# Attention 1 stores undivided columns and sums of exponentials; the division moves to the last stage, and the attention runs in turns of three half tiles

## The chip, the cores and the metric

The kernel runs on one core of a Trainium2 chip. The metric is the device time of one execution in microseconds (us). Three executions of the kernel before took 2754.67, 2756.57 and 2761.1 us; their median, 2756.57, is the time before.

Five engines work at once, each through its own queue in order: TensorE (PE in the profile; PEld are its weight loads), VectorE (DVE), ScalarE (ACT), GpSimd (POOL) and SyncE (SP), which issues all DMAs here. They wait for each other through semaphores only.

## The reference, cut to what matters

```
x = x + xattn_0(layernorm(x), ctx)                 # fake-quantised projections
x = x + ffn_0(layernorm(x))
x = x + xattn_1(layernorm(x), ctx, mask)
x = x + ffn_1(layernorm(x))

def xattn_1(hidden, audio, mask):                  # 16 heads of 32, 4 batches of 512 rows, 1601 context tokens
    q, k, v  = heads(hidden @ Wq.T + bq), heads(audio @ Wk.T + bk), heads(audio @ Wv.T + bv)
    scores   = clip(q k^T / sqrt(32), -50, 50);  -50 where masked
    probs    = softmax(scores);  probs = probs / (probs.sum(-1) + 1e-8)
    ctx      = probs v                              # (4, 512, 512)
    delta    = clip(residual_scale, 0, 0.3) * (ctx @ Wo.T + bo)
    return layernorm(delta) * gamma + beta

def ffn_1(x):   # 8 experts, top 2; every expert has the same weights
    return relu(x @ W_up.T) @ W_down.T + sum(softmax(top2(x @ W_gate.T))) * (x @ W_expert)
```

All is float32 outside and has to be accurate to nearly that; products of float32 are made of three products of high and low parts.

## The kernel before

The program has five stages with a barrier between them: (1) keys, values and queries, (2) attention 0, (3) `ffn_0_and_q_projection_1`, (4) `attention_1`, (5) `out_projection_and_ffn_1`. The change touches stages 3 to 5. The order on every engine is written out by hand; generators (`projected`, `queries`, `closing`) are stepped beside a main loop, one step a `next`, and each engine walks through the same steps.

**Stage 3** (L1366 on) works through 4 batches of 16 slices `f` of the hidden layer. In slice `f` each engine makes `first_half(f + 1)`, steps its side work once, makes `second_half(f)` and steps it once more, so there are 30 steps a batch and a rest after the last. The side work of batch `b` is `projected(b + 1)`, the output projection of attention 0 for the next batch, and `queries(b - 1)`: the norm of the finished rows on DVE into `xn` (in the profile `q_rows`), 16 transposes of `xn` on PE, the split of the transposed rows into parts on ACT and DVE, 12 empty steps, and the query projection of attention 1. On PE and ACT `queries` starts with 6 empty steps; the norm on DVE takes 5 steps and one empty one stands behind it. The PSUM banks of this work (four, `hidden`) are taken in turns, always the one taken longest ago.

**Stage 4**, `attention_1` (L1814), works through 16 units, one for 4 heads of one batch, each of 13 tiles of 128 context tokens (the last has 65). A tile is two halves of 2 heads. For each half PE makes two score products into one of three PSUM windows of two banks (L1905), DVE clips them from PSUM into `probs` (L2009), and ACT takes the exponential in place (L1964). Two tiles later PE multiplies the tile with the values (L1918, four column tiles of 32 into bank `acc`). The sum of exponentials has two ways: for the tiles in `POOLED` (0, 1, 3, 5, 7, 9, 11) POOL adds the whole tile to `pooled` (L2040, six additions a unit), and PE makes one product of `pooled` with ones (L1937); for the six other tiles PE multiplies each with ones (L1931). Six buffers hold `probs`: tile i is clipped only when tile i - 6 has been read by PE and, if it is pooled, by POOL. A unit is closed during the next one: ACT copies `acc` and the sums (L1970, L1971), PE turns the sums into columns (L1883), DVE inverts them with one Newton step (L1986 to L1991), PE spreads the inverses again (L1893), and DVE multiplies (L1998); SP stores the columns to `o_t_1`. SP loads the next unit's keys, queries and values, and in the last unit the weights, rows and columns (`o_first`) of the last stage (`ahead`).

**Stage 5**, `out_projection_and_ffn_1` (L2087), has 4 batches. `projected(b)` splits the attention columns into parts (ACT L2219, DVE L2268), multiplies them with `Wo` on PE (48 products), adds and scales (DVE L2280, L2283), norms, multiplies by gamma and adds the rows (to which POOL has added beta, L2374), and norms again. Each norm has four short DVE instructions on 128x4 elements behind a POOL instruction (`root_on_pool`, L215) and four on 128x512 (L204). `operand(b)` transposes and splits the normed rows; then come gate, up, expert and down products. `projected(0)` and `projected(1)` stand ahead of the loop on PE; on DVE `projected(b + 1)` is stepped beside batch b.

## Time and profile before

| | us |
|---|---|
| median of three executions | 2756.57 |
| the profiled execution, its own time | 2758.67 |
| its span, first to last instruction | 2756.8 |
| PE busy | 2583.9 |
| DVE busy | 1842.0 |
| ACT busy | 1248.4 |
| POOL busy | 1204.4 |

Times in the rows are from the start of the span. A row of the timeline gives start and duration of a run of equal instructions (x8 is eight of them); in brackets stands how long the engine had been idle and who released it. Stage 3 lies between about 1445 and 1934 us, stage 4 from 1934 to 2516 us, stage 5 from there to the end. An f32 product appears as two instructions in the trace. A line number can be that of a helper.

### The profile page before, as it was taken

Reading aid. Unit: us, or ns where it says so; the run is one execution under the profiler, and the core shown is the slowest. Engines: PE = TensorE matmul, PEld = TensorE weight load, DVE = VectorE, ACT = ScalarE, POOL = GpSimd, SP = SyncE. Lnnn points to the kernel's source line nnn. Section 1 sums busy time; section 2 is a strip of 40 time slices with the busy share of each in tenths; the row PEclk is TensorE's granted clock in tenths of the full one; section 3 lists DMA queues with packets and bytes.
Section 4 is the critical chain, followed back from the end, with each engine's and each line's share of the span. In section 5 each row is a group of like instructions: output and inputs, shape, how many; then the busy total and the mean of one; then the engine's idle time right before and its main releaser. Section 6 shows DMA issues by size and latency. Waiting matters only on the chain. (4 is left out here: it accounts for less than half of the span.)

```text
span 2756.8 us, 35478 instructions
## 1 busy us (share of the span) xinstructions
PE 2583.9 (94%) x14009; PEld 1671.8 (61%) x14024; DVE 1842.0 (67%) x2545; ACT 1248.4 (45%) x1869; POOL 1204.4 (44%) x298
## 2 busy tenths in 40 slices
PE   8999999998999999999978998997999999997898
PEld 8888888885444444544426777776333434334776
DVE  5554544456676766767764766553899999997664
ACT  3222312214656565665642222222778778883211
POOL 1000000005999999999940000000677777774110
PEclk9999999999999999999999999999999999998899
DMA  8677666564534435344107534436967777762100
GB/s 294 239 232 258 251 228 246 176 192 116 122 68 93 97 65 121 67 97 93 62 4 256 191 134 164 150 118 167 191 150 152 150 153 150 153 186 100 62 31 31
DMA packets 214855, 400.61 MB, mean 145 GB/s; under 512 B 16696, under 2 KB 92504, under 8 KB 214624
## 3 DMA queue, kind: packets, MB, share of 16 engines
q1 hardware_dynamic: 214688, 398.34, 51.9%
q8 instruction: 111, 1.82, 0.3%
q14 instruction: 56, 0.46, 0.1%
HBM read 256.31 MB, written 140.33 MB: 144 GB/s over the span
## 5 line engine op out<-in xcount | busy, mean ns | idle before, releaser
L1300 POOL TENSOR_TENSOR pooled<-pooled,probs 128x2048 f32<-128x2048 f32 x140 | 641.1, 4579 | 22.1 <-ACT probs L1174 2.5
L1174 ACT ACTIVATE probs<-psum 128x512 f32<-128x512 f32 (+1 forms) x832 | 459.3, 598 | 373.4 <-PE psum L1071 370.4
L1201 DVE TENSOR_REDUCE win_max<-psum 128x1 f32<-128x802 f32 x480 | 453.7, 987 | 169.8 <-PE psum L1036 169.6
L2009 DVE TENSOR_SCALAR probs<-psum,bound 128x1024 f32<-128x1024 f32 (+1 forms) x416 | 507.4, 1277 | 44.5 <-PE psum L1905 44.5
L1964 ACT ACTIVATE probs<-probs 128x1024 f32<-128x1024 f32 (+1 forms) x416 | 440.6, 1059 | 113.3 <-DVE probs L2009 75.4
L2040 POOL TENSOR_TENSOR pooled<-pooled,probs 128x2048 f32<-128x2048 f32 x80 | 368.3, 4604 | 80.5 <-ACT probs L1964 80.5
L1071 PE MATMUL psum<-q_st,k_st 128*128 128x512 f32 (+1 forms) x832 | 336.8, 439 | 36.1 <-ACT den_sb L1186 17.9
L1071 PEld LDWEIGHTS psum<-q_st,k_st 128*128 128x128 f32 (+1 forms) x832 | 149.4, 186 | 258.5 <-ACT probs L1174 175.7
L215 POOL TENSOR_TENSOR r_q<-ve_q,minus_half 128x4 f32<-128x4 f32 x8 | 8.7, 1086 | 669.8 <-DVE ve_q L191 669.8
L1036 PE MATMUL psum<-k_st,q_st 96*128 96x402 f32 x960 | 266.6, 359 | 6.4 <-DVE o_sb L1232 5.2
L1905 PE MATMUL psum<-q_st,k_st 128*128 128x512 f32 (+1 forms) x832 | 250.8, 423 | 11.0 <-PEq L156 10.5
L1905 PEld LDWEIGHTS psum<-q_st,k_st 128*128 128x128 f32 (+1 forms) x832 | 137.4, 185 | 184.3 <-issue 93.5
L1083 PE MATMUL psum<-probs,v_st 128*32 128x512 f32 (+1 forms) x1664 | 222.5, 607 | 0.0
L1036 PEld LDWEIGHTS psum<-k_st,q_st 96*128 96x128 f32 x960 | 174.3, 191 | 61.2 <-DVE win_max L1201 31.6
L168 PE MATMUL psum<-q_st,k_st 128*128 128x512 f32 x576 | 174.4, 397 | 1.5 <-DVE early_v L1631 1.5
L168 PE MATMUL psum<-w,f_g_hi 128*128 128x512 f32 x512 | 165.0, 404 | 10.3 <-DVE f_g_lo L1675 7.3
L1576 ACT ACTIVATE f_code<-f_code 128x512 f32<-128x512 f32 x64 | 40.5, 632 | 288.9 <-DVE f_code L1673 288.9
L1300 POOL TENSOR_TENSOR pooled<-probs 128x2048 f32<-128x2048 f32 x16 | 73.4, 4588 | 198.3 <-ACT probs L1174 198.3
L786 DVE TENSOR_TENSOR v_out<-psum,bv 128x512 f32<-128x512 f32 (+1 forms) x104 | 70.9, 688 | 127.4 <-PE psum L168 115.6
L215 POOL TENSOR_TENSOR r_f<-ve_f,minus_half 128x4 f32<-128x4 f32 x11 | 11.1, 1012 | 328.2 <-DVE ve_f L191 328.2
L168 PE MATMUL psum<-ctx_hi,k_st 128*128 128x400 f32 (+1 forms) x512 | 139.2, 351 | 13.4 <-DVE ctx_lo L758 13.3
L650 ACT ACTIVATE kt_hi<-psum,bk 128x400 fp32r<-128x400 f32 (+1 forms) x128 | 74.6, 595 | 164.2 <-PE psum L168 164.0
(252 smaller groups left out, 4373.6 us busy)
## 6 DMA issues: line engine op xcount, KB each, us to landing
k_st<-k_hi SPq DMA_DIRECT2D x64, 801.0 KB, 11.8
k_st<-k_lo SPq DMA_DIRECT2D x48, 801.0 KB, 11.4
k_hi<-kt_hi SPq DMA_DIRECT2D x32, 801.0 KB, 4.0
k_lo<-kt_lo SPq DMA_DIRECT2D x32, 801.0 KB, 5.8
v_rows<-v_out SPq DMA_DIRECT2D x96, 256.0 KB
v_st<-v_rows SPq DMA_DIRECT2D x24, 768.0 KB
q_st<-q_hi SPq DMA_DIRECT2D x64, 256.0 KB, 11.0
w<-w_hi_d SPq DMA_DIRECT2D x64, 256.0 KB, 3.1
```

Of the source, the lines that this page charges most:

```text
L168: m = M.matmul(dst, lhs, rhs, start=start and n == 0, stop=stop and n == len(terms) - 1)
L650: A.activation(kt_hi[s][:, c0:c0 + cw], bank(kv_banks.where[i])[:, 0:cw], ACT.Identity, bias=bk[n][:, g:g + 1]).then_inc(k_hi_done, 1)
L1036: m = M.matmul(window(slot)[:, w, 0:MW], q_st[s][0:96, j, r * P:(r + 1) * P], k_st[s][0:96, j, start:start + MW], start=True, stop=True)
L1071: M.matmul(bank(slot)[0:rows, :], k_st[s][:, j, t * P:t * P + rows], q_st[s][:, j, :], start=True, stop=True).then_inc(scored, 1)
L1083: m = M.matmul(acc[j * DH:(j + 1) * DH, :], v_st[u % 2][0:rows, t, j * DH:(j + 1) * DH], pr[0:rows, j, :], start=(t == 0), stop=(t == TT - 1))
L1174: A.activation(probs[i % NPROBS][0:rows, j, :], bank(score_banks.where["score", u, t, j])[0:rows, :], ACT.Exp, scale=1.0 / ROOT).then_inc( ...
L1201: V.tensor_reduce(win_max[:, r, j, c:c + 1], window(windows.where["max", u, i])[:, :, 0:MV], AX.XY, ALU.max).then_inc(max_done, 1)
L1300: G.tensor_tensor(pooled[u % 2][:], before[:], probs[tile(u, k) % NPROBS][:], ALU.add).then_inc(pool_added, 1)
L1905: m = M.matmul(ps[0:rows, w, :], k_st[s][:, j + w, t * P:t * P + rows], q_st[s][:, j + w, :], start=True, stop=True)
L1964: A.activation(dst, dst, ACT.Exp, scale=1.0 / ROOT).then_inc(exp_done, 1)
L2009: V.tensor_scalar(probs[i % NPROBS][0:rows, half * W:half * W + W, :], window(("score", u, t, half))[0:rows], bound[0:rows, u // NG, t:t + 1],
L2040: G.tensor_tensor(pooled[:], before[:], this[:], ALU.add).then_inc(pool_added, 1)
```

## The change

It has five parts.

1. **Attention 1 no longer divides.** `closing` is gone on PE and DVE, with `rec`, `unity` and `o_sb`. ACT copies `acc` as soon as the last values product is made (`accumulated`) and the sums after the pooled product, in two places (`ACC_COPY`, `DEN_COPY`) instead of one. SP stores both: the undivided columns to `o_t_1`, the sums (4 rows of 512) to `den_d`. `pooled` has two buffers.
2. **Inverses by batch.** When a batch's four units are stored, SP loads its 8192 sums as 128x64, DVE takes the reciprocal, POOL makes the Newton step (`invert_on_pool`, three instructions), and SP stores them to `rec_d`. This is done for three batches in units 5, 9 and 13 and for the last in stage 5.
3. **Turns of three half tiles.** PE makes the scores of three halves in a row, then one or two value products with their sums (`VALUES`), nine turns a unit instead of 13 tiles of one step each.
4. **Seven pooled additions.** `POOLED` has eight tiles, so POOL makes seven additions a unit and PE five sums and the pooled one. The last unit has five additions and then, on POOL, the multiplication of `o_first` with the loaded inverses.
5. **Last stage and stage 3.** In stage 5 POOL multiplies the columns of batches 1 to 3 with their inverses, which SP loads from `rec_d` spread over 32 partitions each (1 MB a batch, in four DMAs); on DVE the low parts of batch 1 are interleaved with `projected(0)`. In stage 3 the transposes and splits of `queries` come two steps later.

```diff
 # stage 3, queries(b): PE and ACT, and DVE
-                        for _ in range(6):
+                        for _ in range(8):
                             yield
...
                         yield from norm_on_dve(own, nq, rows[b % 2], xn, b, xn_done)
-                        yield
+                        for _ in range(3):
+                            yield
 # new helpers
+        def invert_on_pool(own, cols, done):
+            s = own.after(G.tensor_tensor(cols.den[:], cols.den[:], cols.rec[:], ALU.mult))
+            G.wait_ge(own.sem, s)
+            s = own.after(G.tensor_tensor(cols.den[:], cols.two[:], cols.den[:], ALU.subtract))
+            G.wait_ge(own.sem, s)
+            G.tensor_tensor(cols.rec[:], cols.den[:], cols.rec[:], ALU.mult).then_inc(done, 1)
+        def load_inverses(dst, b, sem):
+            for j in range(HPG):
+                load(dst[j * DH:(j + 1) * DH, :, :], rec_d[b * NG:(b + 1) * NG, j, :].partition_broadcast(DH), sem)
 # attention_1
-            POOLED = [0, 1, 3, 5, 7, 9, 11]
-            FIRST_SUM, LAG, W, NPROBS, CLOSE = 2, 2, 2, 6, 8
+            POOLED = [0, 1, 3, 4, 6, 7, 9, 10]
+            FIRST_SUM, W, NPROBS = 2, 2, 6
+            PER_TURN, ACC_COPY, DEN_COPY = 3, (1, 0), (2, 0)
+            VALUES = [[-2], [-1], [0, 1], [2], [3, 4], [5], [6, 7], [8], [9, 10]]
+                def pooled_tiles(u):
+                    return POOLED if u < UNITS - 1 else POOLED[:-2]
...
+                    for u, k, halves, behind in turns():          # PE
+                        for half in halves:
+                            scores(*half)
+                        for tile_behind in behind:
+                            values(*tile_behind)
+                            sums(*tile_behind)
...
+                    for u, k, halves, _ in turns():               # ACT
+                        for i, half in enumerate(halves):
+                            exps(*half)
+                            if u and (k, i) == ACC_COPY:
+                                copy_acc(u - 1)
+                            if u and (k, i) == DEN_COPY:
+                                copy_den(u - 1)
...
+                    for u, k, halves, _ in turns():               # DVE
+                        for half in halves:
+                            clip(*half)
+                        if k == 0 and inverting(u) is not None:
+                            V.wait_ge(den_landed, 16 * (inverting(u) + 1))
+                            V.reciprocal(cols.rec[:], cols.den[:]).then_inc(divided, 1)
...
+                            if k == 2 and inverting(u) is not None:     # POOL, after the second addition
+                                G.wait_ge(divided, inverting(u) + 1)
+                                invert_on_pool(own, cols, inverted)
+                    G.wait_ge(last.o_landed[0], 16 * NG)
+                    G.wait_ge(last.rec_landed, 16 * HPG)
+                    G.tensor_tensor(last.o_first[:], last.o_first[:], last.rec[:], ALU.mult).then_inc(last.o_normed, 1)
...
-                    Y.wait_ge(o_stored, 16 * UNITS)               # SP, end of the stage
+                    Y.wait_ge(acc_copied, UNITS)
+                    store(o_t_1[UNITS - 1], acc_sb[:], last.stored)
+                    Y.wait_ge(den_copied, UNITS)
+                    store(den_d[UNITS - 1], den_sb[0:P:DH, :], last.stored)
 # out_projection_and_ffn_1
-                        A.wait_ge(o_landed[b % 2], 64 * (b // 2 + 1))
+                        A.wait_ge(last.o_normed, 1 + (b - 1) * NG + 1 if b else 1)
...
-                    for _ in projected(0):                        # DVE
-                        pass
+                    side, next_low = projected(0), low_part(1)
+                    for _ in range(RT):
+                        next(side)
+                        next(next_low, None)
...
+                    def multiplied(b):                            # POOL
+                        G.wait_ge(o_landed[b % 2], 16 * NG * (b // 2 + 1))
+                        G.wait_ge(last.rec_landed, 16 * HPG * (b + 1))
+                        for g in range(NG):
+                            G.tensor_tensor(o_cols[b % 2][:, g, :], o_cols[b % 2][:, g, :], rec[:, g, :],
+                                            ALU.mult).then_inc(last.o_normed, 1)
...
+                    load_rec(1)                                   # SP, ahead of what it loaded before
                     load_o(1)
                     load(rs[:], a["rs"].partition_broadcast(P), rows_given)
                     load(wg_raw[:], a["wg_t"].rearrange("(k p) e -> p k e", p=P), wg_landed)
+                    Y.wait_ge(last.stored, 32)
+                    load(cols.den[:], sums_of(den_d, B - 1), den_landed)
                     load_o(2)
+                    load_rec(2)
```

The first place is PE at the end of a unit and the start of the next in stage 4. `psum<-q_st,k_st` are scores, `psum<-probs,v_st` and `psum<-probs,early_v` values, `psum<-probs,ones` sums of one tile and `psum<-pooled,ones` the pooled sum; the row with 65 is the last tile. Before:

```order
L1905 MATMUL psum<-q_st,k_st 65x512 x4
L1918 MATMUL psum<-probs,early_v 32x512 x4
L1931 MATMUL psum<-probs,ones 32x512 x4
L1905 MATMUL psum<-q_st,k_st 128x512 x4
L1918 MATMUL psum<-probs,early_v 32x512 x4
L1931 MATMUL psum<-probs,ones 32x512 x4
L1937 MATMUL psum<-pooled,ones 32x512 x4
L1905 MATMUL psum<-q_st,k_st 128x512 x4
L1918 MATMUL psum<-probs,v_st 32x512 x4
L1883 MATMUL psum<-ident,den_sb 128x4 x4
L1905 MATMUL psum<-q_st,k_st 128x512 x4
L1893 MATMUL psum<-ident,rec 32x128 x16
```

and now:

```order
L1931 MATMUL psum<-q_st,k_st 65x512 x4
L1944 MATMUL psum<-probs,early_v 32x512 x8
L1931 MATMUL psum<-q_st,k_st 128x512 x6
L1944 MATMUL psum<-probs,early_v 32x512 x4
L1959 MATMUL psum<-probs,ones 32x512 x4
L1931 MATMUL psum<-q_st,k_st 128x512 x6
L1944 MATMUL psum<-probs,early_v 32x512 x4
L1959 MATMUL psum<-probs,ones 32x512 x4
L1965 MATMUL psum<-pooled,ones 32x512 x4
L1931 MATMUL psum<-q_st,k_st 128x512 x6
L1944 MATMUL psum<-probs,v_st 32x512 x8
```

The scores stand in runs of six, the values in runs of up to eight, the two closing products are gone, and the pooled sum stands between the scores of the sixth half of the new unit and those of its seventh.

The second place is POOL from its last addition in stage 4 to the end. `o_cols` are the attention columns, `o_rec` the spread inverses, `r_f` is the root of a norm. Before:

```order
L2040 TENSOR_TENSOR pooled<-pooled,probs 128x2048 x5
L2374 TENSOR_TENSOR f_rows<-f_rows,o_beta 128x512 x4
L215 TENSOR_TENSOR r_f<-ve_f,minus_half 128x4 x2
L2374 TENSOR_TENSOR f_rows<-f_rows,o_beta 128x512 x4
L215 TENSOR_TENSOR r_f<-ve_f,minus_half 128x4 x2
```

and now:

```order
L2040 TENSOR_TENSOR pooled<-pooled,probs 128x2048 x4
L2048 TENSOR_TENSOR o_cols<-o_cols,o_rec 128x2048
L2419 TENSOR_TENSOR f_rows<-f_rows,o_beta 128x512 x4
L2413 TENSOR_TENSOR o_cols<-o_cols,o_rec 128x512 x4
L250 TENSOR_TENSOR r_f<-ve_f,minus_half 128x4 x2
L2413 TENSOR_TENSOR o_cols<-o_cols,o_rec 128x512 x4
L234 TENSOR_TENSOR sums_den<-sums_den,sums_rec 128x64
L236 TENSOR_TENSOR sums_den<-sums_two,sums_den 128x64
L238 TENSOR_TENSOR sums_rec<-sums_den,sums_rec 128x64
L2419 TENSOR_TENSOR f_rows<-f_rows,o_beta 128x512 x4
L250 TENSOR_TENSOR r_f<-ve_f,minus_half 128x4 x2
L2413 TENSOR_TENSOR o_cols<-o_cols,o_rec 128x512 x4
```

Twelve multiplications of 128x512 have come between the instructions that POOL had, four of them directly behind each of the first three norms' pairs and beta additions, and the last inversion stands behind those of batch 2.

## Rows read from the trace of the kernel before

**Rows 1.** Windows: length, then busy us (instructions) of PE, PEld, DVE, ACT, POOL; clock.
```profile
2111.00:2146.00 35.00, 34.75 (x252) 14.09 (x244) 32.17 (x31) 27.92 (x29) 27.02 (x7) 1.00 0.71 153
```
**Rows 2.** Groups of stage 4: line, operation, count, busy us, mean ns, idle before.
```profile
L2009 DVE TENSOR_SCALAR probs<-psum,bound 128x1024 f32<-128x1024 f32 (+1 forms) x416 | 507.4, 1277 | 44.5 <-PE psum L1905 44.5
L1964 ACT ACTIVATE probs<-probs 128x1024 f32<-128x1024 f32 (+1 forms) x416 | 440.6, 1059 | 113.3 <-DVE probs L2009 75.4
L2040 POOL TENSOR_TENSOR pooled<-pooled,probs 128x2048 f32<-128x2048 f32 x80 | 368.3, 4604 | 80.5 <-ACT probs L1964 80.5
```
**Rows 3.** Timeline of one unit of stage 4: start, us, engine, line.
```profile
2145.03 1.20 PE L1905 MATMUL psum<-q_st,k_st 128*128 128x512 f32 x4
2146.16 1.06 PE L1918 MATMUL psum<-probs,v_st 128*32 128x512 f32 x8
2147.16 1.20 PE L1905 MATMUL psum<-q_st,k_st 128*128 128x512 f32 x4
...
2148.29 1.07 PE L1918 MATMUL psum<-probs,v_st 65*32 65x512 f32 x8
2149.17 1.04 PE L1931 MATMUL psum<-probs,ones 65*32 65x512 f32 x8
2150.03 1.04 PE L1937 MATMUL psum<-pooled,ones 128*32 128x512 f32 x8
2151.01 1.20 PE L1905 MATMUL psum<-q_st,k_st 128*128 128x512 f32 x4
...
2151.88 4.87 DVE L2009 TENSOR_SCALAR probs<-psum,bound 128x1024 f32<-128x1024 f32 x4 [1.11 <-PE psum L1905]
...
2153.19 2.25 ACT L1964 ACTIVATE probs<-probs 128x1024 f32<-128x1024 f32 x2 [0.36 <-DVE probs L2009]
...
2155.56 1.05 PE L1883 MATMUL psum<-ident,den_sb 128*128 128x4 f32 x8
...
2180.70 1.20 PE L1905 MATMUL psum<-q_st,k_st 128*128 128x512 f32 x4
```
**Rows 4.** The line of the score products: ns min/median/max of one.
```profile
L1905 PE MATMUL psum<-q_st,k_st x832: 387/397/764, 1933.8 to 2499.6; 128*128 128x512 f32 x154, 128*65 128x512 f32 x13
```
**Rows 5.** Timeline of PE in stage 5: two products in a row.
```profile
2525.33 0.62 PE L168 MATMUL psum<-k_st,o_hi 128*128 128x512 f32 x2
```
**Rows 6.** Timeline of POOL in attention 0, additions back to back.
```profile
1047.20 42.34 POOL L1300 TENSOR_TENSOR pooled<-pooled,probs 128x2048 f32<-128x2048 f32 x9
```
**Rows 7.** Timeline: first transposes of `queries(0)` in stage 3, with PE's wait.
```profile
1587.54 1.94 PE L173 MATMUL psum<-ident,q_rows 128*128 128x128 f32 x8 [4.83 <-DVE q_rows L204]
```
**Rows 8.** Windows of 4 us there, PE alone: length, busy, clock.
```profile
1588.00:1592.00 4.00, 4.00 (x14) 0.50 0.65 206
```
**Rows 9.** Waits of PE between 1640 and 1760 us: total, times, longest.
```profile
PE psum L173 <- DVE q_rows L204: 5.4, 1, 5.4
```
**Rows 10.** Timeline of the end of stage 4.
```profile
2507.46 0.59 ACT L1971 ACTIVATE den_sb<-psum 128x512 f32<-128x512 f32 x1
...
2512.05 0.33 SPq L162 DMA_DIRECT2D o_t<-o_sb  x1
...
2515.70 2.19 ACT L2219 ACTIVATE o_hi<-o_cols 128x512 fp32r<-128x512 f32 x4 [7.65 <-PEq L156]
```
**Rows 11.** Timeline of DVE in stage 5.
```profile
2516.80 2.42 DVE L2268 TENSOR_TENSOR o_lo<-o_cols,o_hi 128x512 fp32r<-128x512 f32 x4
2522.17 6.55 DVE L2268 TENSOR_TENSOR o_lo<-o_cols,o_hi 128x512 fp32r<-128x512 f32 x4 [2.94 <-ACT o_hi L2219]
...
2533.04 0.69 DVE L2280 TENSOR_TENSOR o_delta<-psum,o_bo 128x512 f32<-128x512 f32 x1 [0.67 <-PE psum L168]
```
**Rows 12.** Timeline of POOL in stage 5.
```profile
2521.80 6.37 POOL L2374 TENSOR_TENSOR f_rows<-f_rows,o_beta 128x512 f32<-128x512 f32 x4 [16.02 <-DMA o_rs<-in_rs]
...
2565.61 5.03 POOL L2374 TENSOR_TENSOR f_rows<-f_rows,o_beta 128x512 f32<-128x512 f32 x4 [14.74 <-DMA f_rows<-x_mid]
```
**Rows 13.** One line of DVE between 1300 and 1445 us: ns min/median/max.
```profile
L227 DVE TENSOR_SCALAR f_cols<-f_cols,o_recip x4: 470/472/4649, 1379.4 to 1384.8; 128x512 f32<-128x512 f32 x4
```

More of the change, by code:

```diff
@@ L28 @@
 FT = FF // P
+SUMS = NG * HPG * S // P
 MAGIC = 12582912.0
@@ L1540, in queries @@
                     def queries(b):
-                        for _ in range(6):
+                        for _ in range(8):
                             yield
@@ L2235, in act_program @@
                     A.activation(wg_hi[:, :, 0:NE], wg_raw[:], ACT.Copy).then_inc(wg_hi_done, 1)
+                    for _ in projected(1):
+                        pass
                     operand(0)
```

245 lines of the change are left out of this document (117 added, 128 removed).

## The prediction

> **What bounds the kernel now.** I read the page's busy shares first (PE 94%), then stage 4 in windows, its groups, and one unit of it in the timeline. In a stretch of one unit PE is busy for 34.75 of 35.00 us, at a granted clock of 1.00, the upper level (2.4 GHz), against 32.17 of DVE, 27.92 of ACT and 27.02 of POOL [rows 1]. So PE bounds stage 4, closely followed by DVE.
>
> What PE spends on a unit comes out of the starts in the timeline [rows 3]. Scores of one tile hold PE for 1.13 us until the values start (2145.03 to 2146.16). Values hold it for 0.88 where sums follow (2148.29 to 2149.17) and 1.00 where scores follow (2146.16 to 2147.16), so the way back costs 0.12. Sums of a tile take 0.86 (2149.17 to 2150.03). A product in a row takes 0.23 (0.62 for two, 0.39 for one) [rows 4, 5], four of them 0.92, so 0.21 of the 1.13 is the step from scores to column tiles. A unit is 13 x 1.13 + 13 x 0.12 + 13 x 0.88 + 7 x 0.86 = 33.7, and from 2145.03 to 2180.70, which are the first scores of two units, pass 35.67. The other 1.97 are the two closing products (the first 1.05 in its row) and a short wait for ACT's copy.
>
> DVE's clips follow each other in 1.20 us ((4.87 - 1.28) / 3) [rows 2, 3]: 26 take 31.1. POOL's additions follow each other in 42.34 / 9 = 4.70 [rows 6]; the duration of one is the same in stage 4, 4.60 [rows 2].
>
> **Stage 4, change by change.**
>
> PE: the closings go (-1.97), one sum goes (-0.86), and instead of 13 changes to and fro there are 9 (-4 x 0.33 = -1.3). A unit needs 52 x 0.23 + 9 x 0.33 + 13 x 0.88 + 6 x 0.86 = 31.5 us. DVE needs 31.1; what it had for closing is gone. ACT needs 26 x 1.06 + two copies of 0.59 = 28.7 [rows 2, 10]. POOL needs 7 x 4.70 = 32.9. So what is late next is POOL, 1.4 above PE.
>
> And it can't quite keep that pace. Six buffers hold `probs`; tile 3 of a unit takes the buffer of tile 10 of the unit before, which POOL adds last. Also PE's pooled sum waits for that addition, and the scores of tile 3 stand behind it (the first order rows). From the end of POOL's last addition: 0.05 to the pooled sum, 0.98 to the scores (2150.03 to 2151.01), 0.87 to the clip (to 2151.88), 1.20 to the second clip, 1.31 to its exponential (to 2153.19), about 0.36 because ACT's copy of the sums stands there too, 1.06 + 0.08 until POOL may take tile 3: 5.9 us. POOL meanwhile has the first addition of the new unit, 0.10 + 4.70. So it idles 1.1 a unit, and the unit takes 34.0. DVE and PE have room in all other turns: in a turn of three halves DVE needs 3 x 1.20 = 3.6, and from the end of the last clip PE must give one more pair of scores, two blocks and the next first score: 0.46 + 0.21 + 1.76 + 0.12 + 0.46 + 0.42 = 3.4.
>
> Units 2 to 14: 13 x (35.67 - 34.0) = -21.7. Unit 1 has not yet fallen behind, nor unit 0, which has no closing before either: I take -2 and -1. The inversions stand on POOL between two additions in three units. 128x2048 takes 4.60 and 128x512 1.26 (5.03 / 4) [rows 2, 12], so 0.14 fixed and 0.28 for 64 elements; three with handovers 1.2: +3.6 for three units. DVE's three reciprocals (128x64) stand in DVE's slack, and cost nothing unless POOL holds them up (below).
>
> End: before, unit 15 starts at 2145.03 + 9 x 35.67 = 2466.06, and the next stage starts at 2515.70 [rows 10]: 49.6. Now tile 3 is clipped 10.5 after the unit's start (wait included), 20 more clips take 23.9, the last scores are done at about 32.3, and nine blocks of values and sums (tiles 9 and 10 are summed on PE here) take 7.8: 40.1. The copy ends at 40.9 and the last store is issued; it is no longer waited for. From the issue of the last store to the next stage there passed 3.65 before, landing included (2512.05 to 2515.70); between 1.3 and 3.3 without it, I take 2.0, with the issue 43.3. So -6.3. POOL's multiplication of `o_first` lies in POOL's free time, as the last unit has only five additions.
>
> Stage 4 in sum: -21.7 - 3 + 3.6 - 6.3 = **-27.4**. Bounds: -10 (units at 35.0) and -38 (POOL's 32.9 reached, and the shortest barrier).
>
> **Stage 3.** PE waits for the norm of `queries` 4.83 us at its first transposes [rows 7] and 5.4 a batch later [rows 9]. Behind such a wait the granted clock is 0.50, the lower level (1.2 GHz), for one window of 4 us in which PE was full [rows 8]. In that window half of the work, 2.0 us, is lost; it starts 0.5 after the transposes do and they had begun low, so I take 2.6. Two steps later is one slice later, 24 products of 0.23, 5.5 us of work and so longer than either wait; both go with what the clock costs: -10.2 - 5.2. In the step where the transposes now are, those of `projected` are too, and with four banks the fourth of `queries` needs the bank of the first, so waits for DVE's first split: I work out that it comes 0.3 late, and the next slice's again, 0.5 for each of two batches: +1. Sum **-14.4**; bounds -16 and -5. The last `queries` has nothing beside it and keeps its wait.
>
> **Stage 5.** What DVE does on two SBUF inputs beside POOL is slow: four `o_lo` take 2.42 alone and 6.55 beside POOL's beta additions [rows 11], which themselves take 6.37 instead of 5.03 [rows 12]. So each of DVE's waits for a POOL instruction of 1.26. An operation with one SBUF input does so too: in attention 0 one `f_cols` took 4649 ns against a median of 472, POOL's additions being 4.6 long [rows 13].
> The Trainium skill ("SBUF — State Buffer", SBUF: two separate sides) says why: GpSimd and VectorE share a pair of ports as an exclusive lock that is held for the whole instruction, by VectorE with two SBUF inputs or in a 2-port mode. By that rule stage 5 gives back 12 us as below, without it about 4; the rows agree with the rule.
>
> Start: SP now issues 1 MB of inverses ahead of the 1 MB of columns and the scale, whose row lands at 2521.80 today, 6.1 after the stage's start [rows 12, 10]. Another MB takes no longer than that, and not nothing; I take 3, so 9 after the start. Then POOL has the beta additions (5.0) and the four multiplications of batch 1 (5.0), with DVE's holds to about 20 after the start; ACT's and DVE's parts of groups 0, 1 and 2, 3 stand ahead of the third and fourth rows of `projected(0)`. The fourth row's addition, at 17.3 (2533.04) before, comes at about 22.5: **+5.1** (bounds 2 and 9).
>
> Then POOL multiplies batch 2 directly behind the second norm's root, just when DVE has four short and four long SBUF instructions between PE and its transposes: four POOL instructions of 1.26 hold it, **+5** (0 to 5). The same happens for batch 3 behind the fourth root, in the first loop, where PE has 4 us of work left: **+2** (0 to 5). The later batches have no multiplications. The last batch's inversion ends two loops before it is needed: 0. Sum +12.1, bounds +2 and +19.
>
> **Sum.** -27.4 - 14.4 + 12.1 = -29.7. Against the profiled execution's own 2758.67 that is 2729.0; that execution stands 2.1 above the median, so 2726.9 against 2756.57. I forecast **2727**.
>
> **Rivals.**
> *POOL's tail is short.* The additions end earlier than PE asks, or ACT's copy doesn't stand in the way, and stage 5 gives back only the start: units at 33.2, -10 more, and stage 5 at +5, -7 more: 2711. For it: PE's and DVE's own needs are 31.5 and 31.1. Against: the 4.70 is the mean of nine additions back to back.
> *The last stage takes more.* 3 MB of inverses and 16 multiplications put each batch's start behind, as SP's store and reload of the last inverses stand ahead of the store of the first result: +25 instead of 12: 2740. Against: each of these transfers is issued a batch or more ahead of its use.
> *The turns themselves bind (other side).* The three windows are all refilled within a turn, so DVE waits each turn if the way from clip to scores is longer than I have it. The room is 0.2 a turn by the rows (3.4 against 3.6). If the way is longer by x, a unit takes 26 / 3 turns of 3.4 + x and the pooled sum's 0.9, as POOL then keeps up: 35.6 at x = 0.6, 37.3 at x = 0.8. The whole gets slower than before from 34.0 + 29.7 / 14 = 36.1, so from x = 0.66; at 0.8 it is +46 against the forecast, 2773. For it: in the rows before DVE idles 1.11 at a unit's start. Against: elsewhere it has scores 0.87 after PE starts them.
> *The reciprocals are held by POOL's 4.6 us additions*, as the 4649 ns above: three times up to 4.6, +8 at most: 2735, within the range.
> *The added wait at unit ends drops PE's clock.* PE waits about 1.6 us there. The rows have a drop behind 4.8, and none in the unit start that waits 0.3; nothing between. I give it no case of its own.
>
> **How the numbers follow.** The forecast 0.70; POOL's short tail 0.12; the last stage taking more 0.10; turns binding so far 0.05; a part of it, or of several, that leaves the time where it was 0.03. The likeliest case alone spans 2716 to 2739; the range takes in half of each neighbour: 2711 to 2745. Within 0.2% of 2756.57 (5.5 us) is about what a measurement can't tell from no change; faster by more than that 0.92, the same 0.03, slower 0.05.
>
> **What would show it.** Stage 4: the first scores of two units 34.0 apart; POOL busy 32.3 of 34.0 and idle about 1 before its second addition, released by ACT; PE's pooled sum waiting for POOL by 1 to 2; DVE idle 2 to 2.5 at tile 3. Stage 3: no wait of PE on `q_rows` in two of three batches, and the clock at 1.00 there. Stage 5: DVE's four instructions of the second norm in 5 to 7 us instead of 2, and the first transposes 10 later after the stage's start than before. It is wrong if DVE waits for PE in every turn, or if POOL idles more than 2 a unit.

## The result, and the profile after

The changed kernel takes 2744.20 us (median of 5 runs, 2740.69 to 2747.88), against 2754.67 for the kernel before on the same chip. The medians are 10.5 apart; the ratio, which is that of the means, is 0.9957, 95% interval 0.9943 to 0.9972, which is 12 us. So it is faster by 10 to 12 us, where 30 were forecast. The time lies inside the range 2711 to 2745, at its very end, but the gain is less than half of what the sum said, so the sum was wrong. Between the two traces, which are 14.7 apart, 15 us of the forecast 29.7 are missing, and I look for those.

The profiled executions are 2758.67 before and 2743.92 after: 14.7 apart. Before's is 4.0 above the median of those runs and after's is at its median, which is why the traces differ by more than the medians. With the same four marks in both traces (the last copy of the sums of attention 0, the first score of attention 1, the first `o_hi` of the last stage, the end of the span) the difference is, in the changed kernel:

```profile
1442.26 0.60 ACT L1221 ACTIVATE den_sb<-psum 128x512 f32<-128x512 f32 x1 [1.12 <-PE psum L1139]
...
1926.01 4.49 PE L1931 MATMUL psum<-q_st,k_st 128*128 128x512 f32 x10 [10.44 <-PEq L175]
...
2484.54 0.60 ACT L1993 ACTIVATE den_sb<-psum 128x512 f32<-128x512 f32 x1 [1.12 <-PE psum L1965]
...
2487.94 2.19 ACT L2247 ACTIVATE o_hi<-o_cols 128x512 fp32r<-128x512 f32 x4 [2.80 <-PEq L175]
```

| part | before | after | difference | forecast |
|---|---|---|---|---|
| up to the end of attention 0 | 1443.81 | 1442.26 | -1.6 (no change to the code there) | 0 |
| stage 3 | 490.03 | 483.75 | -6.3 | -14.4 |
| stage 4 | 581.86 | 561.93 | -19.9 | -27.4 |
| stage 5 | 241.1 | 254.2 | +13.1 | +12.1 |

(Before: 1443.81, 1933.84, 2515.70 [rows 10], 2756.8.) Two stages are short by 8.1 and 7.5; the last stage is right within 1.

**Stage 4.** POOL, in the timeline of the changed kernel (start, us, engine, line; in brackets the idle time and what ended it):

```profile
2035.50 4.54 POOL L2040 TENSOR_TENSOR pooled<-probs 128x2048 f32<-128x2048 f32 x1
2042.70 28.35 POOL L2040 TENSOR_TENSOR pooled<-pooled,probs 128x2048 f32<-128x2048 f32 x6 [2.66 <-ACT probs L1981]
2071.00 4.59 POOL L2040 TENSOR_TENSOR pooled<-probs 128x2048 f32<-128x2048 f32 x1
2076.86 4.61 POOL L2040 TENSOR_TENSOR pooled<-pooled,probs 128x2048 f32<-128x2048 f32 x1 [1.27 <-ACT probs L1981]
```

A quiet unit looks as forecast: seven additions, 1.27 idle before the second, released by ACT, and 34.15 from unit to unit (34.0 forecast). But the unit that starts at 2035.50 idles 2.66 there and takes 35.50. What differs is PE's clock. The pooled sum of both units on PE's timeline, and windows of 4 us there (length, busy us of PE, PEld, DVE, ACT, POOL, granted clock):

```profile
2035.59 1.93 PE L1965 MATMUL psum<-pooled,ones 128*32 128x512 f32 x8 [1.65 <-POOL pooled L2040]
...
2071.11 1.06 PE L1965 MATMUL psum<-pooled,ones 128*32 128x512 f32 x8 [1.64 <-POOL pooled L2040]
2072.10 0.73 PE L1931 MATMUL psum<-q_st,k_st 128*128 128x512 f32 x2
```
```profile
2034.50:2038.50 4.00, 2.91 (x11) 1.05 (x12) 0.38 (x1) 1.47 (x2) 4.00 (x2) 0.61 0.85 256
2071.00:2075.00 4.00, 3.89 (x26) 1.62 (x30) 2.03 (x2) 1.19 (x2) 4.00 (x2) 1.00 0.70 206
2105.00:2139.00 34.00, 32.51 (x204) 12.30 (x204) 31.17 (x26) 28.27 (x30) 32.00 (x11) 1.00 0.75 163
```

Both waited the same 1.65 for POOL; behind the one the clock was at the lower level (1.2 GHz) for most of 4 us and the same eight products took 1.93, behind the other 1.06. It fell in 6 of the 15 units in which PE waits there, behind waits of 1.08 to 2.51. Where it falls changes from trace to trace: e1, e4, e5, e6, e7 and e12 below have the same code in this stage, and there, counting units that are more than 0.3 longer than a quiet one, it fell 3 (e1) to 7 (e12) times, once in e1 behind a wait of only 0.95:

```profile
2042.98 1.72 PE L1964 MATMUL psum<-pooled,ones 128*32 128x512 f32 x8 [0.95 <-POOL pooled L2039]
```

The rows say which stretch of a unit is dear: the way from the pooled sum to tile 3's exponential, which POOL waits for.

**Stage 3.** PE no longer waits for `q_rows` in two of the three batches, as forecast. It waits for `g_lo` instead. PE's waits from 1443 to 1925 us (total, times, longest) in the kernel before, and below it in the changed one, then DVE's timeline ahead of one of them:

```profile
PE psum L173 <- DVE q_rows L204: 18.2, 4, 7.8
PE psum L168 <- DVE f_g_lo L1675: 7.3, 7, 1.2
```
```profile
PE psum L187 <- DVE f_g_lo L1711: 12.0, 8, 3.4
PE psum L192 <- DVE q_rows L223: 7.8, 1, 7.8
```
```profile
1574.35 0.69 DVE L1711 TENSOR_TENSOR f_g_lo<-f_code,f_g_hi 128x512 fp32r<-128x512 f32 x1 [1.36 <-ACT f_g_hi L1613]
...
1575.37 1.68 DVE L262 TENSOR_SCALAR f_cols<-f_cols,o_recip 128x512 f32<-128x512 f32 x4
1577.08 1.23 DVE L266 TENSOR_SCALAR f_cols<-f_cols 128x2048 f32<-128x2048 f32 x1
...
1579.01 1.01 DVE L223 TENSOR_SCALAR q_rows<-f_rows,mv_q,r_q 128x512 f32<-128x512 f32 x2
1579.93 0.68 DVE L1704 TENSOR_SCALAR f_code<-psum 128x512 f32<-128x512 f32 x1
...
1583.73 0.70 PE L187 MATMUL psum<-w,f_g_hi 128*128 128x512 f32 x2 [2.79 <-DVE f_g_lo L1711]
...
1585.52 1.05 PE L187 MATMUL psum<-w,f_g_hi 128*128 128x512 f32 x2
```

(The last two rows are PE's.) Between two hidden slices DVE quantises the columns of `projected` and refines and applies the norm of `queries`, from 1574.96 to 1579.93. The next slice's `g_lo` is late by that, and PE waits 2.79; two products behind it take 1.05 instead of 0.62 [rows 5], so the clock is low again, as the window says (its granted clock is the 0.60):

```profile
1584.00:1588.00 4.00, 4.00 (x12) 3.14 (x11) 3.69 (x7) 0.21 (x1) 0.00 (x0) 0.60 0.24 87
```

Before, the `q_rows` waits were 18.2 in all and those for `g_lo` 7.3; now 7.8 and 12.0. The stage's start, where the code is the same, is in these totals. The two batches that the move touches can be taken by themselves: from the 16 transposes of the columns in one batch to those two batches later (1553.46 to 1790.81 before, 1551.70 to 1783.27 now) pass 237.4 before and 231.6 now, 5.8 less. In them 10.2 of `q_rows` waits have gone and 6.2 of `g_lo` waits (8.1 instead of 1.9) have come. That leaves 1.7 for the clock, an estimate by difference, of the 5.2 that I had counted.

**Stage 5.** The fourth `o_delta` starts 23.8 after the stage does (17.3 before), and the refining operations of the second norm, in DVE's timeline:

```profile
2511.78 0.68 DVE L2310 TENSOR_TENSOR o_delta<-psum,o_bo 128x512 f32<-128x512 f32 x1
...
2529.63 1.22 DVE L214 TENSOR_TENSOR t_f<-r_f 128x4 f32<-128x4 f32 x1 [1.12 <-POOL r_f L250]
2530.88 1.18 DVE L216 TENSOR_TENSOR t_f<-t_f,ve_f 128x4 f32<-128x4 f32 x1
2532.10 1.19 DVE L218 TENSOR_SCALAR t_f<-t_f 128x4 f32<-128x4 f32 x1
2533.33 1.18 DVE L220 TENSOR_TENSOR r_f<-r_f,t_f 128x4 f32<-128x4 f32 x1
```

Each of the four takes 1.2 on 128x4 numbers while POOL multiplies columns, from 2529.57 on (e6 below shows that this is the cause). At the first norm, with POOL idle, the same four take 0.16.

### The profile page after: what moved, and what is told of

The parts are those of the page before. It is cut to its first block and busy times, and to the rows that moved or that the text cites. A ratio compares the mean times of both kernels' runs of the same rounds, so it can differ in the third digit from the quotient of the medians.

```text
span 2742.1 us, 34009 instructions
## 1 busy us (share of the span) xinstructions
PE 2544.5 (93%) x13272; PEld 1642.9 (60%) x13272; DVE 1824.8 (67%) x2486; ACT 1241.8 (45%) x1869; POOL 1292.0 (47%) x337
## 5 line engine op out<-in xcount | busy, mean ns | idle before, releaser
L1335 POOL TENSOR_TENSOR pooled<-pooled,probs 128x2048 f32<-128x2048 f32 x140 | 640.8, 4577 | 22.0 <-ACT probs L1209 2.3
L2014 DVE TENSOR_SCALAR probs<-psum,bound 128x1024 f32<-128x1024 f32 (+1 forms) x416 | 499.0, 1274 | 52.5 <-PE psum L1931 52.5
L2040 POOL TENSOR_TENSOR pooled<-pooled,probs 128x2048 f32<-128x2048 f32 x94 | 432.9, 4606 | 35.8 <-ACT probs L1981 25.1
## 6 DMA issues: line engine op xcount, KB each, us to landing
q_st<-q_hi SPq DMA_DIRECT2D x64, 256.0 KB, 10.5
```

Of the source, the lines that this page charges most:

```text
L1335: G.tensor_tensor(pooled[u % 2][:], before[:], probs[tile(u, k) % NPROBS][:], ALU.add).then_inc(pool_added, 1)
L2014: V.tensor_scalar(probs[i % NPROBS][0:rows, half * W:half * W + W, :], window(("score", u, t, half))[0:rows], bound[0:rows, u // NG, t:t + 1],
L2040: G.tensor_tensor(pooled[u % 2][:], before[:], this[:], ALU.add).then_inc(pool_added, 1)
```

## The experiments

All are the changed kernel with one edit, unless said otherwise. Each median is of 4 or 5 executions, e1's of 11. Stage lengths are from the profiled execution of each, with the marks above; that execution can lie off the median (e2's by 5.1 above it, e3's by 4.2 and e5's by 4.8 below, e12's by 4.1 above). With the same code in it, stage 3 took 483.7 to 485.1 and stage 5 252.8 to 254.4, in seven traces each, so a difference there counts from about 1.5 us on. Stage 4 took 559.2 to 562.7 in seven traces, as the clock fell more or less often, so there it counts from about 3.5 us on. The intervals of e5 and e7 overlap the changed kernel's (its executions spread from 2740.69 to 2747.88); what those two show rests on their traces.

| run | median us | ratio to before (95%) | stage 3 | stage 4 | stage 5 |
|---|---|---|---|---|---|
| changed | 2744.20 | 0.9957 (0.9943-0.9972) | 483.8 | 561.9 | 254.2 |
| e1 stage 3 unmoved | 2748.85 | 0.9981 (0.9972-0.9989) | 490.4 | 559.2 | 253.0 |
| e2 sum later | 2720.45 | 0.9880 (0.9867-0.9894) | 485.1 | 539.2 | 254.4 |
| e3 six additions | 2721.67 | 0.9879 (0.9865-0.9892) | 483.7 | 538.5 | 252.8 |
| e4 no multiplications | 2732.84 | 0.9920 (0.9906-0.9933) | 484.5 | 562.4 | 243.5 |
| e5 start order | 2740.00 | 0.9944 (0.9931-0.9956) | 484.5 | 561.1 | 247.9 |
| e6 after norm | 2736.28 | 0.9932 (0.9918-0.9945) | 484.1 | 562.5 | 244.9 |
| e7 spread | 2741.39 | 0.9948 (0.9935-0.9960) | 481.0 | 561.4 | 253.4 |
| e8 all | 2705.22 | 0.9823 (0.9809-0.9836) | 480.5 | 539.0 | 242.1 |
| e9 one score first | 2724.54 | 0.9889 (0.9875-0.9902) | 484.4 | 541.5 | 253.3 |
| e10 | 2707.95 | 0.9828 (0.9815-0.9841) | 481.2 | 539.1 | 244.4 |
| e11 mixed additions | 2700.93 | 0.9803 (0.9790-0.9817) | 480.8 | 532.5 | 241.9 |
| e12 quantise cut | 2735.96 | 0.9929 (0.9916-0.9943) | 476.7 | 562.7 | 254.4 |

**e1: the move in stage 3 undone.**
```diff
 def queries(b):            # PE and ACT
-    for _ in range(8):
+    for _ in range(6):
         yield
...
     yield from norm_on_dve(own, nq, rows[b % 2], xn, b, xn_done)   # DVE
-    for _ in range(3):
-        yield
+    yield
```


> The changed kernel with stage 3's `queries` put back by two steps (6 yields on PE and ACT, 1 on DVE, as before). Theory (the wait moved): with the move, PE no longer waits for `q_rows`, but it waits for `g_lo` instead (9.1 us, 5 times), because DVE's chain of a batch end was the bound all along; the two traces differ in stage 3 by 6.3 us only. Without the move the q_rows waits of 4.8 and 5.4 come back, the g_lo waits fall under 2, the clock in the following window is 0.5 again, and the time rises by 4 to 8 us against the changed kernel: 2748 to 2752. Rival (the move did all that was forecast, 14 us, and something else of the change took 8 back in stage 3): 2758. Rival (stage 3 differs for a reason outside the move): 2744, no difference.

2748.85, 4.7 above the changed kernel, and stage 3 is 490.4, as before (490.0). The waits are back where they were: 18.3 for `q_rows`, 6.4 for `g_lo`. The two batches of above take 237.3, as before (237.4). So the move is all of stage 3's difference, and it is worth 6, not 14.

**e2: the pooled sum later on PE.**
```diff
 for u, k, halves, behind in turns():
     for half in halves:
         scores(*half)
+    if k == 2:
+        pooled_sum(u - 1) if u else None
     for tile_behind in behind:
...
-PER_TURN, ACC_COPY, DEN_COPY = 3, (1, 0), (2, 0)
+PER_TURN, ACC_COPY, DEN_COPY = 3, (1, 0), (2, 2)
```


> The changed kernel with PE's pooled sum of a unit behind the three scores of the next unit's third turn, and ACT's copy of the sums behind that turn's last exponential, instead of the end of the second turn. Theory (the pooled sum's wait ties the loop and drops PE's clock): PE waits 25.0 us for POOL in 15 units, and 6 of the 15 units are 34.7 to 35.5 long with the granted clock at 0.72 to 0.77 there, against 34.15 in the others. With the sum later nothing that POOL needs stands behind it: POOL's idle time before its second addition goes (1.25), the falls of the clock go, units take POOL's 32.9 to 33.1: 14 x 1.1 + 6 = about -20, 2724. Rival (the falls come from the load, not from the wait): the units with a fall remain, and PE then bounds them: -10 to -14, 2732. Rival (POOL really needs 34 a unit): the waits go to DVE (clips waiting for the pooled buffers), the time stays within 4 us of 2744.

2720.45: 24 less, a little more than expected. Its POOL and its PE in the timeline:

```profile
2036.69 4.60 POOL L2044 TENSOR_TENSOR pooled<-probs 128x2048 f32<-128x2048 f32 x1
2041.44 28.36 POOL L2044 TENSOR_TENSOR pooled<-pooled,probs 128x2048 f32<-128x2048 f32 x6
2069.75 4.61 POOL L2044 TENSOR_TENSOR pooled<-probs 128x2048 f32<-128x2048 f32 x1
```
```profile
2036.79 1.06 PE L1966 MATMUL psum<-pooled,ones 128*32 128x512 f32 x8 [0.65 <-POOL pooled L2044]
```

POOL has no idle time left: the units are 33.04 to 33.13, its seven additions, and 33.96 where it inverts. PE still waits for POOL (10.2 us in all, 0.25 to 1.40 each), and not one of the 15 pooled sums took more than 1.07. Both parts of the theory are there: 1.1 a unit from the loop, and the falls. From the first to the last unit's start that is 19.5, and 3.2 more lie in the last unit.

**e3: six additions.**
```diff
-POOLED = [0, 1, 3, 4, 6, 7, 9, 10]
+POOLED = [0, 1, 3, 4, 6, 7, 9]
```
(and for the last unit one tile is left out of it instead of two)

> The changed kernel with six additions on POOL (tiles 0, 1, 3, 4, 6, 7, 9) and tile 10 summed on PE. POOL then needs 28.2 a unit and PE 31.5 + 0.86 = 32.4. Theory: PE does not wait for POOL any more, its clock does not fall, and what is left is PE's own work and the short waits for DVE: units of 33.3 in place of 34.15 to 35.5 (mean 34.5): 14 x 1.2 = -17, 2727. Rival (the falls of the clock come without the wait too): 2733 to 2737. Rival (the longer PE work of a unit is all that counts, since PE was the bound): +0.86 x 15 = 2757.

2721.67, 5 less than expected; units of 33.15 (32.7 to 33.5 around the inversions), no wait of PE for POOL, all 16 pooled sums at 1.04 or 1.05. With 0.86 more work a unit PE gets through it in 1.5 less. The rival that PE's work sets the unit is out by 35 us.

**e9: the pooled sum behind one score instead of three.** The edit is shown against e2; ACT's copy of the sums moves too, to `(2, 1)`.
```diff
-    if k == 2:
-        pooled_sum(u - 1) if u else None
+        if u and (k, i) == (2, 0):      # inside the loop over the halves
+            pooled_sum(u - 1)
```


> The changed kernel with PE's pooled sum behind the first of the three scores of the next unit's third turn (in e2: behind all three). PE still has to wait for POOL there, but a pair of products less: about 1.65 - 0.57 = 1.1 us instead of 1.65, and tile 3's second half and tile 4's first still stand behind it. Theory (a wait of 1.65 drops PE's clock in 6 of 15 units, shorter ones do it less or not): fewer falls, none if 1.1 is short enough, and units of 33.6 to 33.7, since only one of tile 3's two scores stands behind the sum: 2727 to 2731. Rival (the falls don't depend on the length of the wait): still about 6 of 15, 2734.

2724.54, 2.5 below what was expected. The units are 33.1 at once, not 33.6: in what I expected I had taken one product pair off the way to tile 3's exponential, but the first clip (1.20) then also lies ahead of POOL's end; 5.9 - 0.6 - 1.2 is 4.1, less than the first addition's 4.8. PE waits 13 times, 0.15 to 1.50. Eleven sums have waits up to 0.76 or 1.45 and take 1.06 or 1.07; the two behind the longest (1.50 and 1.47) take 1.34 and 1.79, as here:

```profile
2034.05 1.06 PE L1966 MATMUL psum<-pooled,ones 128*32 128x512 f32 x8 [0.59 <-POOL pooled L2044]
...
2267.74 1.79 PE L1966 MATMUL psum<-pooled,ones 128*32 128x512 f32 x8 [1.47 <-POOL pooled L2044]
```

**e4: the last stage without its multiplications.**
```diff
-G.tensor_tensor(o_cols[b % 2][:, g, :], o_cols[b % 2][:, g, :], rec[:, g, :],
+G.tensor_tensor(o_cols[b % 2][:, g, 0:1], o_cols[b % 2][:, g, 0:1], rec[:, g, 0:1],
...
-load(o_cols[b % 2][:, g, :], o_t_1[b * NG + g], o_landed[b % 2])
+load(o_cols[b % 2][:, g, :], q_hi[1][b * NG + g], o_landed[b % 2])
```


> The changed kernel, but in the last stage the columns of batches 1 to 3 are loaded from another DRAM tensor of the same shape (q_hi of attention 1) and POOL multiplies one column of each group instead of 512: the output is not the reference's. Theory (VectorE's small operations are held by GpSimd's 1.2 us multiplications): four operations of 0.16 us took 1.2 each behind the second root and behind the fourth, 4.1 us each time; and the o_lo of batch 1 waited for the multiplications at the start. Without them: -4 behind the second root, 0 to -4 behind the fourth, and -3 to -5 at the start: -8 to -12 in all, about 2734. Rival (the last stage's +13 comes from the transfers of the inverses): -0 to -3, 2742.

This kernel leaves the division of batches 1 to 3 out. Stage 5 takes 243.5 instead of 254.2. So 10.7 of the 13.1 are the multiplications of batches 1 to 3, although POOL is busy with them for 16 us only. The transfers are the same in this kernel, so 2.4 are left for them where nothing waits for a multiplication.

**e6: the same multiplications behind the second norm.**
```diff
 if b + 2 < B:
+    G.wait_ge(normed, b + 1)
     multiplied(b + 2)
```


> The changed kernel where POOL, before it multiplies the columns of batch b + 2, also waits until DVE has finished the second norm of batch b. Same instructions, later. Theory (POOL's instructions of 1.2 us hold DVE's small ones): the four refining operations behind the second and the fourth root take 0.16 instead of 1.2 each, 4.1 us less each time, and what the multiplications then stand beside are DVE's longer ones and its waits for PE: -5 to -8, 2736 to 2739. Rival (the holds only move to the next DVE operations, two SBUF inputs or not): the four small ones are short, but L2330 or the next norm is late by as much: 2743 to 2745.

2736.28, stage 5 at 244.9. The rival falls: the holds don't move elsewhere. DVE's refining operations, which took 1.2 each, and POOL:

```profile
2529.57 0.16 DVE L214 TENSOR_TENSOR t_f<-r_f 128x4 f32<-128x4 f32 x1 [1.12 <-POOL r_f L250]
2529.76 0.16 DVE L216 TENSOR_TENSOR t_f<-t_f,ve_f 128x4 f32<-128x4 f32 x1
...
2532.36 4.96 POOL L2413 TENSOR_TENSOR o_cols<-o_cols,o_rec 128x512 f32<-128x512 f32 x4 [2.82 <-DVE o_delta L223]
```

One semaphore wait on POOL, at a place where nothing needs its products yet, gives 8 us. From the stage's start to the last refining operation of its last norm it is 7.8 less (189.8 instead of 197.5); the other 1.5 of the trace's 9.3 are in the last 55 us, where the code is the same, and not this edit's.

**e5: the small loads first.**
```diff
+load(rs[:], a["rs"].partition_broadcast(P), rows_given)
+load(wg_raw[:], a["wg_t"].rearrange("(k p) e -> p k e", p=P), wg_landed)
 load_rec(1)
 load_o(1)
-load(rs[:], ...)
-load(wg_raw[:], ...)
```


> The changed kernel with SP's two small loads of the last stage (the scale rs and the gate's weights) ahead of the inverses and columns of batch 1 instead of behind them. In the changed kernel the scale lands 11.2 us after the stage's start, POOL's beta additions and its multiplications stand behind it, and the fourth o_delta starts 6.5 later than before. Theory (the scale's landing holds the chain): it lands about 5 us earlier, POOL starts its additions at 6 after the start and is done with both sets 5 us earlier, if batch 1's inverses and columns have landed by then: fourth o_delta -4 to -5, 2740. Rival (the 2 MB of inverses and columns hold it): -1 or less, 2743 to 2744.

2740.00, stage 5 at 247.9. The scale is there 2.5 us after the stage's start instead of 11.2 and the fourth `o_delta` starts at 19.3 instead of 23.8, so 4.5 of the start's 6.5 come from a load of half a KB behind 2 MB. Then the load of the columns is the next bound: POOL's multiplications wait 3.5 for them and start at 11.7 instead of 16.6. That is no contradiction to e4: what waited for the scale were POOL's beta additions, and behind them the multiplications. To the last norm's last refining operation it is 4.7 less, in the whole trace 6.3. (The profiled execution, at 2735.19, is the fastest of its five; I go by the median, -4.2.)

**e7: the norm of `queries` one step later on DVE.**
```diff
+    yield
     yield from norm_on_dve(own, nq, rows[b % 2], xn, b, xn_done)
-    for _ in range(3):
+    for _ in range(2):
         yield
```


> The changed kernel with the norm of stage 3's `queries` one step later on DVE (one yield ahead of it, two instead of three behind it); PE's and ACT's order is unchanged. In the changed kernel DVE has 5.0 us of quantising and norm in one piece between two hidden slices (1574.96 to 1579.93), and PE waits for `g_lo` 0.9 + 2.8 and, a batch later, 0.9 + 3.4. Theory (the wait moved from q_rows to g_lo, because DVE's pieces pile up in one step): spread, the piece is 3.1 and 4.1, the waits together fall from 8.1 to about 4, and the low clock behind them (1584.5 to 1588.1) goes too: -4 to -7, 2738 to 2740. Rival (DVE's whole work in those steps is the bound, however it is spread): the waits move to the next slice, -1 to +1, 2744.

Stage 3 is 2.8 shorter (the two batches 3.3), the median 2.8 lower: in the direction of the theory, but less than expected. The same edit is in e8, e10 and e11, and stage 3 is 480.5 to 481.2 there too. The waits at the two places are 0.5 + 1.4 + 0.9 and 0.5 + 2.0, 5.3 instead of 8.1: they shrink and spread, and one of 0.6 for a bank comes in, so the rival is right in part.

**e12: DVE's quantising cut.** Three of its four steps work on one column of 512:
```diff
-yield from quantise_on_dve(own, cols, step, recip, o_coded)
...
+    s = own.after(V.tensor_scalar(cols[:, k, 0:1], cols[:, k, 0:1], recip[:, k:k + 1], 127.0,
+                                  ALU.mult, ALU.min))
...
+s = own.after(V.tensor_scalar(cols[:, :, 0:1], cols[:, :, 0:1], -127.0, MAGIC, ALU.max, ALU.add))
...
+V.tensor_scalar(cols[:, :, 0:1], cols[:, :, 0:1], MAGIC, None, ALU.subtract).then_inc(o_coded, 1)
```


> The changed kernel, but in stage 3 three of the four steps in which DVE quantises the attention columns of `projected` work on one column of 512 (lines 262, 266, 269; the reduction stays): the output is not the reference's. It takes 1.7 + 1.2 + 1.2 = 4.1 us from DVE between the hidden slices of each batch, and nothing from PE. Theory (what is left in stage 3 is PE waiting for `g_lo`, as DVE's quantising and the moved norm lie in one step): the g_lo waits 0.9 + 2.8 and 0.9 + 3.4 fall to under 1 each pair, the low clock behind them goes, and stage 3 (483.75 from the last copy of attention 0 to the first score) loses 6 + 3 = 9: about 475, whole time 2735. Rival (PE waits for something else as soon as that is gone): under 3, 2741 or more.

2735.96, stage 3 at 476.7: 7.0 less, by taking 4.1 us a batch from DVE and nothing from PE. PE at the four places:

```profile
1577.67 0.70 PE L187 MATMUL psum<-w,f_g_hi 128*128 128x512 f32 x2 [0.97 <-DVE f_g_lo L1727]
1584.07 0.71 PE L187 MATMUL psum<-w,f_g_hi 128*128 128x512 f32 x2 [0.65 <-DVE f_g_lo L1727]
1689.42 0.71 PE L187 MATMUL psum<-w,f_g_hi 128*128 128x512 f32 x2 [0.95 <-DVE f_g_lo L1727]
1696.41 0.70 PE L187 MATMUL psum<-w,f_g_hi 128*128 128x512 f32 x2 [1.23 <-DVE f_g_lo L1727]
```

Stage 3 is then 13.3 shorter than before (the two batches too), close to the 14.4 that I had counted as if DVE had nothing else to deliver. In the two batches 8.3 of that are waits and so about 5 the clock's, as forecast. So most of the missing 8 of stage 3 is DVE's. What the move alone would be worth with the quantising cut isn't shown: the kernel with the cut and without the move was not run, and it may be faster than before as well.

**e8, e10, e11: put together.** e8 is e2, e5, e6 and e7, and in addition
```diff
 for _ in range(RT):
     next(side)
-    next(next_low, None)
```


> All of it together on the changed kernel: the pooled sum later (2720.5 by itself), the small loads first, POOL's multiplications behind the second norm, the norm of `queries` spread, and DVE's o_lo of batch 1 behind all four o_delta of batch 0 instead of between them. Theory: the parts lie in different stages and add: 2720.5 - 4 - 6 - 5 - 3 = 2702. Rival (the edits of the last stage don't pay): 2713 to 2716.

> e8 without its edit of DVE's o_lo of batch 1 (they stand again between the o_delta of batch 0). In e8 the last stage took 242.1 against 254.2 in the changed kernel, where e5 and e6 by themselves took 6.3 and 9.3 off. Theory (the o_lo behind the o_delta push the norm back, as DVE waits there for POOL's multiplications): the last stage takes 254.2 - 6.3 - 9.3 = 238.6 and the whole 2705.2 - 3.5 = 2701.7. Rival (the two savings overlap): 2705.

> e10 with six additions on POOL instead of seven in the three units in which POOL inverts (units 5, 9, 13); PE sums that tile. Theory (POOL bounds at 33.06 a unit, 33.95 with the inversion): these units come down to PE's 33.1, and their saved addition lets POOL run ahead in the next ones, which PE and DVE then bound at 32.5 to 32.9: -3 to -5 against e10. Rival (PE's extra sum and the fixed order cost as much): -1 to +1.

e8 takes 2705.22: the parts of stages 3 and 4 add, those of the last stage (242.1) don't add in full. I put that down to e8's own edit and took it out in e10; that was wrong, e10 takes 2707.95 and its last stage 244.4. With the same code e11 has 241.9 there, so the edit can't be told from nothing. From the stage's start to the last refining operation of the last norm the changed kernel takes 197.5, e5 192.8, e6 189.8, e8 187.0, e10 186.6 and e11 186.7. What follows is the same code and takes 56.6, 55.1, 55.1, 55.1, 57.8 and 55.1: PE's clock falls there in the first (0.63 in one window of 4 us) and in e10 (0.67), not in the others. So the savings of e5 and e6, 4.7 and 7.8, overlap by about 2 only; once the scale is early, the chain at the start waits for PE and, 3.5 us, for batch 1's columns. The rest of what seemed to be missing is that clock.

e11 is the fastest, 2700.93, 7.0 under e10 and 54 under the kernel before. Its edit:
```diff
+if inverting(u) is not None:
+    return POOLED[:-1]
```
The three units with an inversion fall from 33.95 to 31.39, more than I expected: POOL is spared an addition of 4.7 exactly where it has 0.9 extra, and what it ran late by is made up. The units behind them stay at 33.1; that POOL would run ahead there and shorten them did not come.

```profile
2097.85 4.61 POOL L2047 TENSOR_TENSOR pooled<-probs 128x2048 f32<-128x2048 f32 x1
...
2129.24 4.61 POOL L2047 TENSOR_TENSOR pooled<-probs 128x2048 f32<-128x2048 f32 x1 [2.09 <-ACT probs L1988]
```

## Why the prediction was wrong, step by step

**"Units 2 to 14: 13 x (35.67 - 34.0) = -21.7" was too much.** The mechanism (POOL's loop through the pooled sum, idle 1.1 a unit) is right: quiet units take 34.15, idle 1.27, and e2 takes the loop away and gets POOL's 33.1. From the two traces units 2 to 14 gained 13.6, inversions included, against -21.7 + 3.6. The quiet unit is 0.15 longer than forecast (2 us), the falls of the clock cost 3.6 there (estimated as what those units are longer than quiet ones), and the inversions cost 0.86 each instead of 1.2 (1 better).

**"I give it no case of its own" is the step that failed in stage 4.** I had a wait of 4.8 that drops the clock and one of 0.3 that doesn't, and a new wait of 1.6 in every unit, and read "nothing between" as nothing. It was an unknown between two bounds and should have been priced: 0 at one end, and at the other 15 units with 2.0 us of work lost in each, as in [rows 8], 30 us on a way that POOL waits for. It came to about 4.4 us in the 15 intervals of the profile, and 1.4 in the last unit. e3 without the wait has no fall, and e2, e8 and e10 with waits of up to 1.40 have none; e9 has two. So the falls come with the wait, but its length doesn't decide by itself: 1.64 left the clock up in one unit of the changed kernel and not in another, and 0.95 was followed by a fall in e1. What else decides stays open.

**"Unit 1 -2, unit 0 -1" had the wrong sign for unit 0.** It went from 32.26 to 33.11, and unit 1, a fall of 0.8 in it, from 35.73 to 34.94. I thought of a unit that has not yet fallen behind PE; but POOL's seven additions are its pace from the first unit, where before six left room. -3.0 forecast, +0.1 measured.

**The end of stage 4 (-6.3) was right by luck**: from the last unit's first addition to the next stage pass 42.7 before and 36.3 after, but one of the six falls lies in it. In e1, e4, e6, e7 and e12, with the same code and no fall there, it is 35.0, so the end was worth -7.7, and the fall took 1.4 of it back.

**"Both go with what the clock costs: -10.2 - 5.2" is the step that failed in stage 3.** The q_rows waits did go. The order rows showed DVE's order unchanged up to the norm, and I asked only whether `q_rows` would be ready one slice later. I did not ask what DVE's 5 us piece makes late besides `q_rows`: the hidden slice behind it. Before, PE stood at the transposes and so never reached `g_lo` early; the wait for `q_rows` hid that for `g_lo`. By e1 the move is worth 5 to 6.6; with DVE's quantising cut as well (e12) the stage is 13.3 shorter than before; by e7 spreading returns 2.8. The +1 for the new bank waits did not come: the transposes at 1590.95 and 1591.39 have none.

**Stage 5 (+12.1) was right in sum and about right in its parts**: start +6.5 (5.1), the second norm +4.1 (5), the rest +2.5 (2). The rest is no clean term: at the fourth norm the holds come again (+4.1, 15 in sum) and about 2 come back behind it. e4 and e6 show the cause that the prediction gave. The Trainium skill ("SBUF — State Buffer", SBUF: two separate sides) calls the ports that GpSimd and VectorE share an exclusive lock, held for the whole instruction. The rows agree (four operations of 0.16 at 1.2 each while POOL's instructions are 1.2 long, 0.16 again in e6), and they show it for `t_f<-t_f` too, which reads a single tensor; the page has that case for a 2-port mode, and no run here shows in which mode the operation ran.

**The profile of before.** I took 2.1 off for its distance to the median; in the second set of five it was 4.0. That is most of the difference between the 14.7 of the traces and the 10.5 of the medians, and nothing of the missing 15.

**Rivals.** "The last stage takes more" gave 2740 and comes nearest, but for the wrong reason: that stage is as forecast. "The turns themselves bind" is out: e2's DVE waits 5.9 us for PE in all of stage 4. "POOL's tail is short" is out as well, POOL idles 1.27. "The reciprocals are held" is out: DVE's three take 0.54 us each. The one that happened is the last, the clock, to which I gave neither a case nor a price; the rest are two terms of the sum.

## What to carry to other kernels

A wait that is taken away can have hidden another on the same engine, as in stage 3: before a gain is booked, list what else the late engine delivers in the same step, and when. Where an order is written by hand, put the product that waits for the slowest engine behind the work that this engine itself will need next; that cost nothing here and was worth 24 us, twice what the whole change was. And a multiplication on an idle POOL isn't free while DVE has many short operations that read SBUF (four of 0.16 took 1.2 each here); one semaphore that holds POOL back was worth 8.

## What the runs showed of the hardware that I had not expected

- PE's granted clock fell behind waits of 1.08 to 2.51 us in a stretch where PE is otherwise 95% busy, in 6 of 15 equal places of one trace (two waits of 1.65 and 1.64: once 1.93, once 1.06 for the same eight products). One such fall made the unit up to 1.35 longer. Behind 14 waits of 0.25 to 1.40 (e2) it did not fall, and behind one of 0.95 (e1) it did. The same code had 3 to 7 falls in seven traces, and stage 4 was 559.2 to 562.7 long.
- DVE's operations on 128x4 numbers take 1.2 us each beside POOL's 1.25 us multiplications of 128x512; four of them are over after 4.9 us, alone after 0.8, so 4.1 later.
- POOL's three inversions of 128x64 take 0.32 to 0.33 each and cost 0.86 a unit together, with their semaphores.
